# Attention of sixteen 8-wide heads: from one head over 128 rows to stacks of four heads by 32 rows

## The reference

```
mod = silu(c) @ wmod                      # six rows of 128 per batch: sa ca ga sb cb gb
h   = layernorm(x) * (1 + ca) + sa
Q, K, V = h @ W.T  as 16 heads of 8;  Q, K rotated by position
p   = softmax(causal(Q K^T / sqrt(8)))
x   = x + ga' * ((p V) @ W_O.T)           # ga' = sign * max(|ga|, 0.25)
h   = layernorm(x) * (1 + cb) + sb
x   = x + gb' * ffn(h)                    # ffn: rms norm, top 2 of 8 experts, 128 -> 512 -> 128 with silu(a) * b
```

## Time and profile before

| | us |
|---|---|
| median of 3 runs (608.49 to 610.49) | 609.79 |
| the profiled execution | 609.25 |
| its span | 607.4 |
| TensorE / VectorE / ScalarE / GpSimd busy | 479.3 / 461.9 / 422.7 / 343.0 |
| attention pipeline | about 20 to 378 |
| experts, last sums | about 380 to 605 |

### The profile page before, as it was taken

How to read it: one execution, slowest core, us unless ns; L and a number is a source line. 1 busy time by engine, 2 the same in 40 slices (tenths; PEclk the granted TensorE clock), 3 DMA queues, 4 the chain that set the end, 5 groups by cost and what they waited for, 6 DMA issues and landing times.

```text
span 607.4 us, 19940 instructions
## 1 busy us (share of the span) xinstructions
PE 479.3 (79%) x5529; PEld 380.5 (63%) x5530; DVE 461.9 (76%) x1571; ACT 422.7 (70%) x1108; POOL 343.0 (56%) x501
## 2 busy tenths in 40 slices
PE   4579997889888988888899751199999999999500
PEld 1356775667666766666677530198888888888400
DVE  5576889889888988898988455277877777778456
ACT  3458876878787878777886632088888888898500
POOL 5443455767676767677765466214555545545553
PEclk9989999999999999999999875599999999999755
DMA  8321122211221232112211030512212211111076
GB/s 236 83 72 36 42 55 59 63 47 57 75 64 41 54 78 61 39 56 78 60 41 43 31 94 27 121 42 57 66 51 56 61 48 53 55 53 46 19 229 186
DMA packets 53668, 41.53 MB, mean 68 GB/s; under 512 B 7554, under 2 KB 48341, under 8 KB 53616
## 3 DMA queue, kind: packets, MB, share of 16 engines
q1 hardware_dynamic: 43056, 29.12, 18.2%
q0 software_dynamic: 4544, 8.54, 4.4%
q10 hardware_dynamic: 6016, 3.24, 1.9%
HBM read 24.80 MB, written 12.78 MB: 62 GB/s over the span
## 4 chain that ended last, share of the span: by engine, by line
PE 53%; DVE 23%; issue 9%; DMA 5%; ACT 5%; POOL 3%; DVEq 1%; SPq 1%; ACTq 0%; POOLq 0%
DVE nmax L797 5%; PE bank L1319 5%; PE bank L1127 5%; PE bank L1162 5%; PE bank L1320 4%; PE bank L1321 4%; PE bank L1340 3%; PE bank L1341 3%; PE bank L1342 2%; PE bank L1140 2%; PE bank L1151 2%; PE bank L1139 2%; PE bank L1165 2%; PE bank L1177 2%; PE bank L1115 2%
## 5 line engine op out<-in xcount | busy, mean ns | idle before, releaser
L797 DVE TENSOR_REDUCE nmax<-bank 128x3 f32<-128x384 f32 x256 | 139.0, 550 | 26.2 <-PE bank L1127 24.3
L1127 PE MATMUL bank<-cb,c 128*128 128x256 bf16 x512 | 141.5, 276 | 0.0
L602 ACT ACTIVATE probs<-bank 128x384 f32<-128x384 f32 x256 | 124.0, 496 | 21.1 <-PE bank L1127 19.5
L555 POOL DMA_INDIRECT expert_outs<-probs,number_of x78 | 78.8, 1011 | 92.5 <-ACT probs L705 79.3
L1037 DVE SCALAR_TENSOR_TENSOR probs<-bank,b_sb,probs 128x256 f32<-128x256 f32 x156 | 71.7, 480 | 52.2 <-ACT probs L716 52.0
L1319 PE MATMUL bank<-xt,we_hi 128*128 128x256 f16 x312 | 86.0, 276 | 2.1 <-issue 0.8
L1320 PE MATMUL bank<-xt,we_hi 128*128 128x256 f16 x312 | 85.8, 275 | 0.0
L1321 PE MATMUL bank<-xt,we_lo 128*128 128x256 f16 x312 | 85.8, 275 | 0.0
L696 ACT ACTIVATE hh<-probs 128x256 f16<-128x256 f32 x156 | 64.1, 411 | 18.9 <-DVE probs L1037 16.4
L469 POOL DMA_INDIRECT expert_rows<-send,pos_i x64 | 63.5, 992 | 24.2 <-issue 12.4
L1151 PE MATMUL bank<-q_max,k_pad 128*128 128x256 f16 x256 | 70.8, 277 | 1.1 <-ACT probs L602 1.0
(11 more groups left out here) (179 smaller groups left out, 1326.9 us busy)
## 6 DMA issues: line engine op xcount, KB each, us to landing
g_in<-expert_rows SPq DMA_DIRECT2D x39, 132.0 KB
k_pad<-qk_t SPq DMA_DIRECT2D x128, 32.0 KB, 1.9
mod_b<-mod_rows SPq DMA_DIRECT2D x16, 256.0 KB, 3.2
we_lo<-expert_outs SPq DMA_DIRECT2D x16, 256.0 KB, 3.6
wstage<-in_L_ffn_W1a_dram SPq DMA_DIRECT2D x16, 128.0 KB, 2.4
wstage<-in_L_ffn_W1b_dram SPq DMA_DIRECT2D x16, 128.0 KB, 2.5
wstage<-in_L_ffn_W_dram SPq DMA_DIRECT2D x16, 128.0 KB, 2.7
out_dram<-we_lo ACTq DMA_DIRECT2D x16, 128.0 KB, 3.2
```

The source lines that it names most:

```text
L555: pool.indirect_dma_start(out=outs, out_offset=bass.IndirectOffsetOnAxis(ap=number_of[:, r, s:s + 1], axis=0), in_=y_sb[:, r, s, :], in_of ...
L602: nc.scalar.activation(probs[:, k % (2 * HG)], col_bank[k % 2][:, 0:S + P], ACT.Exp, scale=SM_SCALE).then_inc(probs_ready, 1)
L797: nc.vector.tensor_reduce(nmax[:, k], row_bank[k % 2][:, 0:3 * P].rearrange("p (c t) -> p c t", t=P), AX.X, ALU.max, negate=True).then_inc ...
L1127: return mm(diagonal, ident16, mask.unsqueeze(1).broadcast_to([P, 2, P]), start=False, stop=True, skip_group_check=True)
```

## The change

- Scores are formed per head on 32 rows and in 32 by 32 pieces of weights: a product takes one chunk of 32 queries (or keys) of one head as weights, on rows 32g to 32g+31 of both input and output, and streams the keys before it (or the queries behind it), so causality goes in steps of 32. Four heads of a group j lie on four row and column quarters, hence "stacks". `k_pad` and its copies go; the query pass (K = 24 rows) reads `qk_t` directly.
- By query there are 11 units (`BY_QUERY`) of two chunks and one to four groups, by key 12 units (`BY_KEY`) of 384 columns; the pipeline has 12 steps in place of 16. Masks are 32 by 32.
- The maxima (four heads in the partitions, 32 queries each) are turned by VectorE's 32 by 32 transpose into `nmax_t`, and 16 DMAs a batch (`place_max`) write them to rows 24 to 31 of each slot, one row per chunk; the keys have ones in all eight rows and the queries zeros elsewhere.
- Value products are per chunk of 32 keys, 32 by 32, for two groups into two banks `o_pair`; the odd group writes one quarter further, and the projection weights are permuted to match. Values are projected straight into the stacked layout (`project_values`).
- All projections run as 32-bit products with `w_t` in place of three half-precision ones; the copies and differences of the high and low parts go. The rotation is three instructions in place of six.
- One `chain` bank carries the s0, routing and ranking chains. The choice of experts moves into the next iteration's first two steps, ranking to its third step, placing to steps 2 to 7. The low parts of the expert weights move to the head of GpSimd's iteration.
- The pipeline is written out without a hardware loop; `qk_t` and `v_aug` have three buffers.

```diff
+NC = S // SLOT
+
+BY_QUERY = [((0, 1), (0, 1, 2, 3)), ((2, 3), (0, 1)), ((4, 5), (0,)), ((4, 5), (1,)), ((6, 7), (0,)), ((6, 7), (1,)),
+            ((2, 3), (2, 3)), ((4, 5), (2,)), ((4, 5), (3,)), ((6, 7), (2,)), ((6, 7), (3,))]
+NQ, HALF_Q = len(BY_QUERY), 6
+
+BY_KEY = [((0, 0), (4, 256)), ((1, 0), (3, 224)), ((2, 0), (5, 192), (6, 288), (7, 352))]
+KCOLS = 384
+NK = HG * len(BY_KEY)
+AT_CHUNK = {c: KCOLS * u + off for u, unit in enumerate(BY_KEY) for c, off in unit}
...
-        qk_t = sb("qk_t", [P, 2, 2 * HG, S], F16)
-        k_pad = sb("k_pad", [P, 2, H, S], F16)
-
-        nmax = sb("nmax", [P, H, 3])
-        q_max = sb("q_max", [P, 2, HG, S], F16)
-        v_aug = sb("v_aug", [P, 2, NS, H, SLOT])
-
-        probs = sb("probs", [P, 2 * HG, S + P])
+        qk_t = sb("qk_t", [P, 3, 2 * HG, S], F16)
+
+        nmax = sb("nmax", [P, HG, SLOT], F16)
+        nmax_t = sb("nmax_t", [P, 2, HG, SLOT], F16)
+        v_aug = sb("v_aug", [P, 3, NC, HG, SLOT])
+
+        probs = sb("probs", [P, HG, len(BY_KEY) * KCOLS])
...
+        o_pair = ctx.enter_context(nc.psum_tensor("o_pair", [P, 2, 512], F32))
+        chain = ctx.enter_context(nc.psum_tensor("chain", [P, 512], F32))
+        tail_bank = ctx.enter_context(nc.psum_tensor("tail_bank", [P, 512], F32))
...
-                    sp.wait_ge(act0.sem, act0.after(b, "ev1_keys"))
-                        for g in range(HG):
-                            at = slice(SLOT * g, SLOT * g + SLOT)
-                            heads = k_pad[at, par, :, :].rearrange("p (j g) t -> p j g t", g=HG)[:, 2 * half:2 * half + 2, g, :]
-                            sp.dma_start(heads, qk_t[at, par, HG + 2 * half:HG + 2 * half + 2, :]).then_inc(pad_in[half][par][g], 16)
...
+            def place_max(b, half):
+                sp.wait_ge(max_turned, 2 * b + half + 1)
+                js = slice(2 * half, 2 * half + 2)
+                for c in range(NC):
+                    row = slice(3 * DK + c, P, SLOT)
+                    sp.dma_start(qk_t[row, b % 3, js, SLOT * c:SLOT * c + SLOT], nmax_t[row, b % 2, js, :]).then_inc(max_in[half][b % 2], 16)
...
-                    nc.gpsimd.tensor_tensor(ht_lo[:], ht32[:], ht_hi[:], ALU.subtract).then_inc(pool0.sem, 1)
...
-                        nc.scalar.activation(probs[:, k % (2 * HG)], col_bank[k % 2][:, 0:S + P], ACT.Exp, scale=SM_SCALE).then_inc(probs_ready, 1)
...
+                        nc.scalar.activation(probs[:, k // 3, KCOLS * (k % 3):KCOLS * (k % 3) + KCOLS], col_bank[k % 2][:, 0:KCOLS], ACT.Exp, scale=SM_SCALE).then_inc(probs_ready, 1)
...
+            def save_pair(b, pair):
+                act.wait_ge(probs_used, NC * (2 * b + pair + 1))
+                nc.scalar.activation(o_t[:, b % 2, 2 * pair:2 * pair + 2, :], o_pair[:, :, 0:S], ACT.Copy).then_inc(group_saved, 1)
...
+            def max_of(b, u):
+
+                chunks, js = BY_QUERY[u]
+                seg = SLOT * chunks[1] + SLOT
+                vec.wait_ge(rows_ready, HG * (NQ * b + u + 1))
+                if u == 0 and due(b):
+                    vec.wait_ge(max_turned, 2 * b)
+                scores = row_bank[(b + u) % 2][:, 0:2 * seg * len(js)].rearrange("p (j c t) -> p j c t", c=2, t=seg)
+                nc.vector.tensor_reduce(nmax[:, js[0]:js[-1] + 1, 3 * DK + chunks[0]:3 * DK + chunks[1] + 1], scores, AX.X, ALU.max, negate=True).then_inc(max_ready, 1)
+
+            def turn_max(b, half):
+                js = slice(2 * half, 2 * half + 2)
+                vec.wait_ge(max_ready, NQ * b + (HALF_Q, NQ)[half])
+
+                if due(b // 2):
+                    vec.wait_ge(max_in[half][b % 2], 16 * NC * (b // 2))
+                nc.vector.transpose(nmax_t[:, b % 2, js, :].rearrange("p j w -> p (j w)"), nmax[:, js, :].rearrange("p j w -> p (j w)")).then_inc(max_turned, 1)
...
+                if part == 0:
+                    vec.wait_ge(pe0.sem, pe0.after(b, "proj"))
+                    nc.vector.tensor_tensor(turn_c[:].rearrange("p s h (u w) -> p s (h u) w", w=w), chain[:].rearrange("p (s h w) -> p s h w", s=NS, w=w),
+                                            cos.unsqueeze(2).broadcast_to([P, NS, 4 * H, w]), ALU.mult).then_inc(vec0.sem, 1)
+                    sines(b, 0, qk)
+                else:
+                    sines(b, 1, qk)
+
+            def sines(b, s, qk):
+                nc.vector.tensor_tensor(turn_s[:, s].rearrange("p h (u w) -> p h u w", u=2), qk[:, s, :, ::-1, :],
+                                        sin[:, s].unsqueeze(1).broadcast_to([P, 2 * H, 2, DK // 2]), ALU.mult).then_inc(vec0.sem, 1)
...
-            def low_out(b):
-                vec.wait_ge(act3a.sem, act3a.after(b, "on_hi"))
-                nc.vector.tensor_tensor(on_lo[:], tail_bank[:, 0:S], on_hi[:], ALU.subtract).then_inc(vec3a.sem, 1)
...
-            def project(b, s):
-                at = slice(P * s, P * s + P)
-                o = (chain_b, chain_a)[s][:, 0:3 * D]
-                halves(o, ht_hi[:, at], ht_lo[:, at], w_hi[:, 0:3, :].rearrange("p n d -> p (n d)"), w_lo[:, 0:3, :].rearrange("p n d -> p (n d)")).then_inc(pe0.sem, 1)
+            def project(b):
+                for s in range(NS):
+                    t = mm(chain[:, S * s:S * s + S], ht32[:, P * s:P * s + P], w_t[:, 0:2, :].rearrange("p n d -> p (n d)"), start=(s == 0), stop=True, skip_group_check=True)
+                t.then_inc(pe0.sem, 1)
+
+            def project_values(b):
+                columns = w_t[:, 2].rearrange("p (j g w) -> p j g w", g=HG, w=DK)
+                for c in range(NC):
+                    for g in range(HG):
+                        o = tail_bank[SLOT * g:SLOT * g + SLOT, SLOT * c:SLOT * c + SLOT].rearrange("p (j w) -> p j w", w=DK)
+                        t = mm(o, ht32[:, SLOT * c:SLOT * c + SLOT], columns[:, :, g, :], start=(c == 0), stop=True, skip_group_check=True)
+                        if c == NC - 1:
+                            t.then_inc(v_ready, 1)
...
+            def scores_by_query(b, u):
+                chunks, js = BY_QUERY[u]
+                seg = SLOT * chunks[1] + SLOT
+                if u == 0:
+                    pe.wait_ge(act0.sem, act0.after(b, "ev0"))
+                if u == 1:
                     pe.wait_ge(act0.sem, act0.after(b, "ev1"))
+                if due(NQ * b + u - 1):
+                    pe.wait_ge(max_ready, NQ * b + u - 1)
+                bank = row_bank[(b + u) % 2]
+                for n, j in enumerate(js):
+                    for m, c in enumerate(chunks):
+                        at = seg * (2 * n + m)
+                        for g in range(HG):
+                            rows_g = slice(SLOT * g, SLOT * g + 3 * DK)
+                            mm(bank[SLOT * g:SLOT * g + SLOT, at:at + SLOT * c + SLOT], qk_t[rows_g, b % 3, j, SLOT * c:SLOT * c + SLOT],
+                               qk_t[rows_g, b % 3, HG + j, 0:SLOT * c + SLOT], start=(n == 0 and m == 0), stop=False, skip_group_check=True)
+                for g in range(HG):
+                    group = slice(SLOT * g, SLOT * g + SLOT)
+                    last_keys = bank[group, 0:2 * seg * len(js)].rearrange("p (j c t) -> p j c t", c=2, t=seg)[:, :, :, seg - 2 * SLOT:]
+                    mask = mask_q[group].rearrange("p (c t) -> p c t", c=2).unsqueeze(1).broadcast_to([SLOT, len(js), 2, 2 * SLOT])
+                    mm(last_keys, ident16[group, group], mask, start=False, stop=True, skip_group_check=True).then_inc(rows_ready, 1)
             def scores_by_key(b, k):
+                j, unit = k // 3, BY_KEY[k % 3]
+                if k % 6 == 0:
+                    pe.wait_ge(max_in[k // 6][b % 2], 16 * NC * (b // 2 + 1))
+                if due(NK * b + k - 1):
+                    pe.wait_ge(probs_ready, NK * b + k - 1)
+                bank = col_bank[k % 2]
+                for n, (c, at) in enumerate(unit):
+                    for g in range(HG):
+                        group = slice(SLOT * g, SLOT * g + SLOT)
+                        mm(bank[group, at:at + S - SLOT * c], qk_t[group, b % 3, HG + j, SLOT * c:SLOT * c + SLOT], qk_t[group, b % 3, j, SLOT * c:],
+                           start=(n == 0), stop=False, skip_group_check=True)
+                pairs = [unit[n:n + 2] for n in range(0, len(unit), 2)]
+                for n, ((_, at), (_, next_at)) in enumerate(pairs):
+                    for g in range(HG):
+                        group = slice(SLOT * g, SLOT * g + SLOT)
+                        first_queries = bank[group, at:at + 2 * (next_at - at)].rearrange("p (c t) -> p c t", c=2)[:, :, 0:SLOT]
+                        t = mm(first_queries, ident16[group, group], mask_k[group].unsqueeze(1).broadcast_to([SLOT, 2, SLOT]), start=False, stop=True, skip_group_check=True)
+                        if n == len(pairs) - 1:
+                            t.then_inc(cols_ready, 1)
+            def values(b, pair, chunks):
+                if chunks[0] == 0:
+                    if due(2 * b + pair):
```

(43 more changed lines are left out.)

577 lines of the change are left out of this document (223 added, 354 removed).

## The result

The changed kernel takes 660.23 us (median of four runs, 656.16 to 662.12), the kernel before 609.14 beside it (606.49 to 610.49): a ratio of 1.084, with a 95% interval of 1.081 to 1.088. The forecast was 576. I sum against the profiled execution, 656.16 us with a span of 654.3.

A forecast was written before the change was run, and what follows sets the result against it. TensorE and VectorE were both taken to bound the kernel, TensorE deciding afterwards. The period falls from 20.36 to 18.3 us, 31.5 us over 15.3 periods, and the front gains 2: 609.25 - 31.5 - 2 = 576 us, range 540 to 645.

The forecast's parts named there:

- the idle time of TensorE: Steady period: waits for `member` go, those for the maxima shrink; 0.8 us left for the chain bank at the period's end.
- the unrolled program: Batches written out lengthen the program; instruction fetches were priced at nothing, up to 0.5 us a period.
- TensorE's work: Steady period: streams, starts and changes of shape of TensorE's products sum to 17.5 us, where it was 17.8.
- The first rival, starts bind: Small products on TensorE need 30 ns instead of 10: about 727 us, chance 0.14; slower beyond some 15 ns.
- The floor of about 25 ns from start to start: Skill page's limit on TensorE products, cited against the change: by it 684 small products cost 17 us alone.
- The 4 ns of its Part 3: Skill page's start spacing for tiles of TensorE's array: small stacks would be pure streaming, about 1 us a period lower.
- Value products on eight tiles: Value products on TensorE run on eight tiles at once, 4.3 us a period; with four at a time 8.3.
- VectorE: Steady period: fewer reductions, placements and rotation instructions bring VectorE from 18.2 to 15.4 us.
- ScalarE: Steady period: fewer exponentials and copies bring ScalarE from 16.0 to 11.4 us.
- Transfers: 16 tiny DMAs of the maxima per batch land in time, with slack of 2.4 and 4.3 us.
- The front: Before the first exponentials: the first query scores need no key copies, 2 us gained.
- Removed waits: Rank products and choice of experts move within the period, so TensorE's 1.3 us behind `member` go.

The follow-up runs named there:

- projections: Kernel before with 16-bit values, plus 32-bit projections and the two-instruction rotation: 589.75 us, ratio 0.969; with the 16-bit values alone 590.62 us.
- the second bank in three kernels: Second-half transposes moved to a free value-product bank: changed kernel 660.46 us; that with 16-bit values 626.50; that with scores as whole-array products 603.37.

## Why the prediction was wrong, step by step

**The step that failed** is the idle time of TensorE, "I leave 0.8 us", with the sentence on the unrolled program beside it, "its fetches have no row of their own at this rate and I take nothing, up to 0.5 us a period". The period missed its 18.3 us by 5.8: 1.9 of work and 3.9 of idle time, which measured 4.7. 2.6 of these 4.7 us stand at the ends of instruction blocks (3.1 from start to start, as above). I had seen that the program grows; what I did not work out is the rate: some 1460 instructions in 18 us would be a block each 3.2 us, as fast as blocks ever came here, with nothing spare for the dense stretches; at the 3.7 us of the stops 5.7 blocks are 21 us. The page of the kernel before has the block size (26 loads of the instruction queue, 0.43 MB), and the count of new products was mine. How fast blocks can come it does not show, for there no two loads are closer than 7.4 us. The other 2.1 us are mostly the named waits: the chain bank and the state behind it, for which I had left 0.8, took 1.5, and the divided output, which I had not named, 0.4.

**TensorE's work** was forecast at 17.5 us and measured 19.4. From one product's start to the next, idle time taken off, per batch: query scores 3.4 (forecast 3.0), key scores 3.6 (2.7), values 5.3 (4.3), value projection 0.8 (0.6); small products 13.0 us for 684, 19 ns each, against 10.6. All other work took 6.3 against 6.85. In this count a change of shape falls to the product before it. The key masks, 64 in 1.3 us, show it: some 0.9 us of that is the way to the first product of another shape, 0.12 us behind the last mask of a stack, seven times a batch. Of the 1.9 us, 0.5 is the part of the stops that counts as work, I estimate 0.5 for the clock, 0.96 where I took 1.00, and the value products are 1.0 over, which in part holds the other two.

The first rival, starts bind, had the size about right (the small ones passed the 12.7 us at which it turns slower) but not the mechanism. The 19 ns are an average that holds streaming, changes of shape and part of the stops. Inside a stack the starts are closer than the 10 ns that I took. A key mask stack, and the durations of its products (shortest, middle, longest):
```profile
158.40 0.20 PE L1143 MATMUL bank<-cb,c 32*32 32x64 bf16 x4
L1143 PE MATMUL bank<-cb,c x1024: 183/187/257, 39.7 to 398.1; 32*32 32x64 bf16 x171
```
Four products of 187 ns end within 0.20 us, so their starts lie some 4 ns apart. That is the middle value over all score and mask stacks; of the 32-bit products those of the values stand 10 ns apart in the middle, those of the value projection 7 (41 start within 0.4 us, 9 ns each on average). By work alone, with 0.8 idle, the period would have been 20.2, about even. The floor of about 25 ns from start to start, which the Trainium skill gives (TensorE: Matmul & The Clock Gate, Part 1), does not hold for these tiles: a load and its product took 19 ns on average over whole batches. The 4 ns of its Part 3 agree with the score and mask stacks; the sum did not come down by it, because what lies between the stacks decides.

**Value products on eight tiles** was right. All of them took 5.3 us a batch, where four tiles at a time would take 8.3. The 48 instructions of the longest chunks (256, 224 and 192 columns, two stacks of heads each) would take 2 x 672 x 1.8 ns = 2.4 us by four tiles and 1.2 by eight. The rows:
```profile
161.75 0.42 PE L1158 MATMUL o_pair<-probs,v_aug 32*32 32x256 f32 x4
161.82 1.31 PE L1158 MATMUL o_pair<-probs,v_aug 32*32 32x256 f32 x44
```
They took 1.4 us with the way through the array. The 80 of the shorter chunks would take 1.7 or 0.9 us; one row has them in 1.2:
```profile
142.19 1.19 PE L1158 MATMUL o_pair<-probs,v_aug 32*32 32x160 f32 x80
```

**VectorE** was forecast at 15.4 and measured 16.3. The edits were priced well; the grouped rows between 100 and 340 us, by shape:
```profile
L782 DVE TENSOR_REDUCE nmax<-bank 128x2 f16<-128x512 f32 x40 | 27.7, 692 | 30.4 <-PE bank L1123 30.3
L782 DVE TENSOR_REDUCE nmax<-bank 128x2 f16<-128x384 f32 x40 | 22.0, 551 | 5.6 <-PE bank L1123 5.4
L745 DVE TENSOR_SCALAR ve<-mv 128x2 f32<-128x2 f32 x20 | 11.2, 562 | 0.3
```
All reductions came to 7.0 us a batch, as forecast (0.145 + 512 x 0.00105 = 0.683 for the first form); the two 32 by 32 transposes to 245 ns each where I took 250. The excess is in lines that nobody edited, such as the last, 319 ns over the ten batches of the kernel before. Since VectorE is no bound after, this moved nothing.

**ScalarE** was forecast at 11.4 and measured 12.9. I left out that the key and query tiles are now one copy of 1024 columns instead of 512:
```profile
L645 ACT ACTIVATE qk_t<-chain 128x1024 f16<-128x1024 f16 x21 | 21.6, 1028 | 1.0
L653 ACT ACTIVATE o_t<-o_pair 128x512 f32<-128x512 f32 x20 | 11.8, 592 | 0.0
```
Two at 1.03 us instead of 0.60, 0.9 us a batch, and it is just this copy for which TensorE waits at the chain bank. The second row is the copy that I had at 600.

**Transfers** were right: no wait stands on the maxima. **The front** was wrong: the first exponential came at 40.4 us, 1.1 later than before, not 2 earlier.

**Removed waits.** `member` is gone from TensorE's waits, as forecast. What that gave by itself no run shows; the idle time as a whole grew.

What stays open: how much of the 3.1 us would come back if blocks were always in time with nothing else changed. No kernel here does that; the nearest, scores as whole-array products, also has 2.4 us less work. Why the value products took 1.0 us more than eight tiles would need is open too. And why the clock sank to 0.87 with 16-bit values while the kernel before with 16-bit values kept 0.99 is not settled.

## What to carry to other kernels

When a change cuts work into small pieces, count the instruction blocks of a period before pricing any product, divide the period by them, and compare with the shortest distance between loads on the instruction queue in a trace that has dense stretches. Price small products from hundreds in a row, with what stands between their stacks, not from a burst of sixteen. Where no engine is full, a removed wait or a relieved engine gives back little: four such edits here (projections, and the second bank in three kernels) gave 0 to 5 us.

## What the runs showed of the hardware that was not expected

- In these traces TensorE's instructions came in blocks of 256 (16 KB), at least 3.2 us apart. At the 35 stops the load began 0.8 to 1.8 us after the block place before, and TensorE went on 2.2 to 3.1 us after that. It stopped in the middle of a stack, and the profile calls it "issue".
- An instruction that waits for a semaphore already reached takes 106 ns of TensorE's sequencer in both kernels. 16 ns of it showed in the time where long products stream, and 71 among small stacks, where the clock also fell to 0.77.
- One visit of whole-array work among small stacks cost 0.1 us (2.7 us for 27, net of the products saved).
- 32 by 32 products of a score or mask stack start 4 ns apart; over hundreds, with streams and changes of shape, it is 19 ns each. 32-bit stacks on eight tiles run together (48 instructions in 1.4 us).
